# One core, attention, memory read and routed experts: row maxima written as the softmax shift, full-height bias products, expert numbers read a step earlier

## What is computed

```python
x = x + attn_a(layernorm(x))     # 16 query heads, 4 key groups, head size 16, causal softmax
x = x + ffn(layernorm(x))        # router, top 2 of 8 experts, 256 -> 176 -> 256
x = x + attn_b(layernorm(x))     # linear attention read from 4 memory banks
x = x + ffn(layernorm(x))        # the same experts again
```

```python
q = xh @ wq + bq ; k = xh @ wk + bk ; v = xh @ wv + bv     # biases are not zero
q, k = rmsnorm(q), rmsnorm(k)                              # then rotary embedding
logits = einsum(q, k) * head_scale ; causal mask
probs = softmax(logits) ; out = einsum(probs, v) @ wo + bo
```

## Time and profile before

| | us |
|---|---|
| median of 3 runs | 573.01 (572.78 to 574.89) |
| the profiled execution, its own time | 568.61 |
| its span, from first to last instruction | 566.8 |
| PE busy | 498.1 (88%) |
| DVE busy | 375.0 (66%) |
| ACT busy | 269.2 (47%) |
| POOL busy | 248.7 (44%) |

### The profile page before, as it was taken

The page is one execution under the profiler, slowest core; times in us unless marked ns, Lnnn a source line. Parts: engine busy times, 40 slices in busy tenths (PEclk is TensorE's granted clock), DMA queues, the critical chain, the costliest instruction groups (busy, mean ns, idle before and its releaser), DMA issues. The chain is left out here.

```text
span 566.8 us, 10974 instructions
## 1 busy us (share of the span) xinstructions
PE 498.1 (88%) x3374; PEld 336.2 (59%) x3374; DVE 375.0 (66%) x1098; ACT 269.2 (47%) x642; POOL 248.7 (44%) x308
## 2 busy tenths in 40 slices
PE   6899999889959969969999989999999787899970
PEld 2455666646736746746777656575667465677740
DVE  5989999779848936654443738766987373344473
ACT  4568998658846843423333333534134222233320
POOL 5329283466150052464243466237663453423440
PEclk9989999979988988989999988999999797999995
DMA  6480601110120231444323393212142244333496
GB/s 213 177 344 29 168 12 58 57 37 13 55 82 6 77 112 38 134 158 140 94 87 108 124 175 52 34 39 103 58 133 75 81 143 140 118 98 98 130 288 202
DMA packets 43736, 60.77 MB, mean 107 GB/s; under 512 B 5856, under 2 KB 38240, under 8 KB 43040
## 3 DMA queue, kind: packets, MB, share of 16 engines
q1 hardware_dynamic: 33152, 37.72, 21.9%
q0 software_dynamic: 9984, 21.83, 12.7%
q10 hardware_dynamic: 544, 0.52, 0.3%
HBM read 28.89 MB, written 25.00 MB: 95 GB/s over the span
## 5 line engine op out<-in xcount | busy, mean ns | idle before, releaser
L1917 POOL DMA_INDIRECT ys<-yo,xin x78 | 75.9, 973 | 126.3 <-DVE yo L1739 117.6
L1176 PE MATMUL PS<-wexp,xTt 128*128 x312 | 110.9, 483 | 8.5 <-ACT xTt L1382 6.8
L1518 DVE TENSOR_REDUCE smax<-PS 128x1 f32<-128x512 f32 (+3 forms) x176 | 103.2, 634 | 13.7 <-remote 7.9
L1344 ACT ACTIVATE prob<-PS 128x512 f16<-128x512 f32 (+1 forms) x176 | 92.1, 563 | 29.1 <-remote 13.3
L1902 POOL DMA_INDIRECT xs<-xn,pos x64 | 62.4, 976 | 59.0 <-DVE pos L1613 42.5
L1193 PE MATMUL PS<-wexp,hT 88*128 x312 | 83.6, 397 | 5.4 <-issue 3.0
L1726 DVE SCALAR_TENSOR_TENSOR sg<-th,PS 128x176 f32<-128x176 f32 x78 | 26.2, 336 | 80.6 <-ACT th L1388 65.3
L1176 PEld LDWEIGHTS PS<-wexp,xTt 128*128 128x128 f32 x312 | 56.9, 198 | 34.2 <-issue 13.7
L1388 ACT ACTIVATE th<-PS 128x176 f32<-128x176 f32 x78 | 24.7, 317 | 107.7 <-PE PS L1176 81.1
L1063 PE MATMUL PS<-qT,kbd 128*128 128x512 f16 (+3 forms) x256 | 63.7, 307 | 13.1 <-issue 7.6
L1193 PEld LDWEIGHTS PS<-wexp,hT 88*128 88x128 f32 x312 | 57.0, 197 | 18.0 <-issue 8.9
(11 more groups left out here) (210 smaller groups left out, 855.9 us busy)
## 6 DMA issues: line engine op xcount, KB each, us to landing
xin<-xs SPq DMA_DIRECT2D x78, 129.0 KB
wexp<-in_experts SPq DMA_DIRECT2D x4, 1216.0 KB, 9.1
kbd<-ys SPq DMA_DIRECT2D x18, 256.0 KB
xs<-zeros SPq DMA_DIRECT2D x32, 129.0 KB
xn<-xn SPq DMA_DIRECT2D x8, 512.0 KB, 3.4
xall<-ys POOLq DMA_DIRECT2D x6, 512.0 KB, 5.9
out<-xall SPq DMA_DIRECT2D x8, 256.0 KB
kbd<-kT SPq DMA_DIRECT2D x60, 32.0 KB, 1.9
```

What stands on the lines that cost most here:

```text
L1176: mm = pe.matmul(PS[:, bank, 0:2 * FI], xTt[:, j % NXT, kc * P:(kc + 1) * P], wexp[:, bass.ds(expert[f, j], 1), kc * 2 * FI:(kc + 1) * 2 * FI]
L1344: act.activation(prob[:, u % NPR, 0:nr * w], PS[:, bank, 0:nr * w], ACT.Exp, scale=ATT_SCALE)\
L1518: dve.tensor_reduce(smax[:, i, REP * g + r0:REP * g + r0 + nr], PS[:, bank, 0:nr * w].rearrange("p (r w) -> p r w", r=nr), AX.X, ALU.max). ...
L1917: pool.indirect_dma_start(ys[f], bass.IndirectOffsetOnAxis(xin[:, j % NXIN, D + 1:D + 2].bitcast(I32), axis=0), yo[:, j % NYO], None).then ...
```

## The change

1. The row maxima are written by the reduction itself, as float16, into column HD of `qa`. The step `shift`, its semaphore and `smax` are gone, and so is column HD + 1. So that the value fits, ScalarE scales the transposed queries by 1/16 in its copy to `qT1`, and the keys hold -16.0 in one column.
2. `shiftedT` waits for the 11 reductions of its group directly, by `out_of` for each unit.
3. The bias products take 128 rows: `top_h` (row 0 ones, the others zero) by a bias tile of 128 rows.
4. The registers with the expert numbers are loaded by `name_experts`: at the first tile of a stage ahead of `xT`, otherwise behind the `gate_up` before the fourth.
5. POOL's presets write `top_h` (two memsets instead of one), and one key column instead of two; `clear` clears one column.
6. The planner loses the `shift` steps; its costs of `qkv`, `project` and `gate_up` on PE are smaller; NUDGE has new values throughout, so that the orders of all engines are new.

```diff
-NUDGE = {("add", 0): 0.2, ("apply", 0): -0.8, ("apply", 1): 25.7, ...
+NUDGE = {("add", 0): 79.9, ("apply", 0): 24.9, ("apply", 1): -16.5, ...
...
-        w.add(PE, r(), 0.69, "qkv", b, i, ...
+        w.add(PE, r(), 0.5, "qkv", b, i, ...
...
-        w.add(DVE, t, 0.5, "shift", b, g, after=[(DVE, "first", b, g, n) for n in range(NU)],
-              behind=[(DVE, "shift", *divmod(NG * b + g - 1, NG))] * (b + g > 0))
         last = NG * b + g - 2
-        w.add(PE, t, 0.23, "shiftedT", b, g, after=[(DVE, "shift", b, g)]
+        w.add(PE, t, 0.23, "shiftedT", b, g, after=[(DVE, "first", b, g, n) for n in range(NU)]
...
-        w.add(PE, r(), 1.05, "project", b, n, ...
+        w.add(PE, r(), 0.66, "project", b, n, ...
...
-    w.add(PE, t(0), 1.19 + 0.3 * ((j - STAGES[n][1]) % 4 == 0), "gate_up", f, j, ...
+    w.add(PE, t(0), 1.19, "gate_up", f, j, ...
...
+                def name_experts(f, j):
+
+                    n = stage_of(j)
+                    i = j - STAGES[n][1]
+                    if i == 0:
+                        pe.wait_ge(plan_ready, (LAST + 1) * f + n + 1)
+                    for k, v in enumerate(nc.values_load_multi_w_load_instructions(
+                            plan[0:1, PLAN_E[n] + i:PLAN_E[n] + i + 4], ...
+                        expert[f, j + k] = v
...
-                        pe.matmul(PS[:, bank, 0:QKV], ones_h[0:1], bqkv_h[0:1], start=False, stop=True)\
+                        pe.matmul(PS[:, bank, 0:QKV], top_h[:], bqkv_h[:], start=False, stop=True)\
...
-                        pe.wait_ge(shift_ready, NG * b + g + 1)
+                        for n in range(NU):
+                            out_of(pe, "first", b, g, n)
                         bank = room(pe, kind, b, g)
...
-                            mm = pe.matmul(o, ones_h[0:1], bo_h[0:1], start=False, stop=True)
+                            mm = pe.matmul(o, top_h[:], bo_h[:], start=False, stop=True)
...
+                        if j == STAGES[stage_of(j)][1]:
+                            name_experts(f, j)
                         pe.wait_ge(xin_loaded[j % NXIN], 16 * loads_of(f, j))
...
                         mm.then_inc(filled[bank], 1)
+                        n = stage_of(j)
+                        if (j + 1 - STAGES[n][1]) % 4 == 0 and j + 1 < STAGES[n][2]:
+                            name_experts(f, j + 1)
...
-                                       bank16(bank)[:, 0:len(groups) * S], ACT.Copy).then_inc(taken[bank], 1)
+                                       bank16(bank)[:, 0:len(groups) * S], ACT.Copy, scale=1.0 / SHIFT)\
...
-                        dve.tensor_reduce(smax[:, i, REP * g + r0:REP * g + r0 + nr],
+                        dve.tensor_reduce(qa[:, b % 2, i, REP * g + r0:REP * g + r0 + nr, HD],
                                           PS[:, bank, 0:nr * w].rearrange("p (r w) -> p r w", r=nr),
                                           AX.X, ALU.max).then_inc(taken[bank], 1)
-                    elif kind == "shift":
-                        ...
-                        link(dve.tensor_scalar(qa[:, b % 2, :, hs, HD], smax[:, :, hs], -1.0 / SHIFT, None, ALU.mult))
-                        dve.scalar_tensor_tensor(qa[:, b % 2, :, hs, HD + 1], smax[:, :, hs], -1.0 / SHIFT,
-                                                 qa[:, b % 2, :, hs, HD], ALU.mult, ALU.subtract)\
-                           .then_inc(shift_ready, 1)
...
-                        pool.memset(ones_h[:], 1.0)
+                        pool.memset(top_h[:], 0.0)
...
-                        pool.memset(ka[:, :, :, HD:HD + 2], SHIFT)
+                        pool.memset(top_h[0:1], 1.0)
+                        pool.memset(ka[:, :, :, HD:HD + 1], -SHIFT)
...
-                        pool.tensor_copy(bqkv_h[:], first["bqkv"][0:1]).then_inc(bias_ready, 1)
+                        pool.tensor_copy(bqkv_h[:], first["bqkv"]).then_inc(bias_ready, 1)
```

More of the change, by code:

```diff
@@ L89 @@
 OUTPUT_BANKS = (5, 6)
[L94 to L129, removed]
-         ("values", 1): 268.5, ("values", 2): 1.7, ("values", 3): -8, ("weigh", 0): -29.6, ("weigh", 1): 21.5,
-         ("wgt", 0): 13.6, ("wgt", 3): 48.1, ("xT", 0): 304.5, ("xT", 1): 14.6}
@@ L280, in front @@
     for i in range(NT):
-        w.add(PE, r(), 0.69, "qkv", b, i, after=[(DVE if h else ACTE, "f_turn", b, h) for h in range(len(halves(b)))]
+        w.add(PE, r(), 0.5, "qkv", b, i, after=[(DVE if h else ACTE, "f_turn", b, h) for h in range(len(halves(b)))]
               + [(ACTE, "constants"), (POOL, "bias"), (POOL, "presets")]
@@ L372, in back @@
     for n in range(2):
-        w.add(PE, r(), 1.05, "project", b, n, after=[(ACTE, "outT", b), (ACTE, "out_weights")], behind=[(PE, "project", b, 0)] * n, banks=m,
+        w.add(PE, r(), 0.66, "project", b, n, after=[(ACTE, "outT", b), (ACTE, "out_weights")], behind=[(PE, "project", b, 0)] * n, banks=m,
               emptied=(DVE, "project", b, n))
@@ L965, in _ @@
                 expert = {}
+                def name_experts(f, j):
[4 more added lines that the diff above has]
+                    for k, v in enumerate(nc.values_load_multi_w_load_instructions(
+                            plan[0:1, PLAN_E[n] + i:PLAN_E[n] + i + 4], engines=[mybir.EngineType.PE], min_val=0, max_val=NE - 1,
+                            skip_runtime_bounds_check_because="the plan names one of the experts")[1]):
+                        expert[f, j + k] = v
                 for kind, *a in ORDER[PE]:
@@ L1161, in _ @@
                         f, j = a
-                        n = stage_of(j)
-                        i = j - STAGES[n][1]
-                        if i == 0:
-                            pe.wait_ge(plan_ready, (LAST + 1) * f + n + 1)
-                            if j == 0 and f == 0:
-                                pe.wait_ge(experts_loaded, 16 * NE // 2)
-                        if i % 4 == 0:
-                            for k, v in enumerate(nc.values_load_multi_w_load_instructions(
-                                    plan[0:1, PLAN_E[n] + i:PLAN_E[n] + i + 4], engines=[mybir.EngineType.PE], min_val=0, max_val=NE - 1,
-                                    skip_runtime_bounds_check_because="the plan names one of the experts")[1]):
-                                expert[f, j + k] = v
+                        if j == 0 and f == 0:
+                            pe.wait_ge(experts_loaded, 16 * NE // 2)
                         out_of(pe, "xT", f, j)
@@ L1331, in _ @@
                         act.activation(qT1[:, b % 2, groups[0]:groups[-1] + 1].rearrange("p g s -> p (g s)"),
-                                       bank16(bank)[:, 0:len(groups) * S], ACT.Copy).then_inc(taken[bank], 1)
+                                       bank16(bank)[:, 0:len(groups) * S], ACT.Copy, scale=1.0 / SHIFT)\
+                           .then_inc(taken[bank], 1)
                     elif kind == "shiftedT":
@@ L1881, in _ @@
                             pool.wait_ge(presets, 2)
[L1882 removed]
+                        pool.memset(qa[:, b % 2, :, :, HD:HD + 1], 0.0).then_inc(cleared, 1)
                     elif kind == "late":
```

56 lines of the change are left out of this document (43 added, 13 removed).

## The result

| | us |
|---|---|
| before, median (572.78 to 574.89) | 572.89 |
| after, median of 4 runs (556.12 to 597.45) | 560.26 |
| ratio, 95% interval | 0.9754 (0.9709 to 0.9798) |
| forecast, and its range | 567.0 (557 to 577) |
| profiled execution after, its own time and span | 559.93, 558.1 |

The run of 597.45 was a disturbed one and is not in the ratio. The gain is 12.6 us by these medians and 14.1 by the ratio, where 6.0 were forecast: the direction and the range hold, but the forecast size is less than half of what came. The two traces are 8.7 us apart, since the traced execution of before was 4.4 us under its median. What follows compares times by ratios to the kernel before on the same chip, because chips differ (the median of before was 566.05 on one and 572.63 on another).

The account below looks back on a forecast made before the run. VectorE was taken to bound the scores, TensorE the expert rounds' gate/up products. 4.1 + 1.8 + 0.6 (shift) + 1.1 (bias) - 1.6 (waits) = 6.0 us, so the median 573.0 becomes 567.0, range 557 to 577.

Parts of the forecast that it names:

- The bound: Scores from 35 to 105 us: VectorE sets the pace at 96% busy, ScalarE next; TensorE's 67.81 us flatters it.
- Rival A: From 35 to 158 us TensorE or ScalarE already paces, absorbing freed time: gain 1, 572 us; chance 0.22 together with D.
- The shift step: VectorE's queue gets back 9.9 us; on the path 4.1 (35 to 105 us), 1.8 (120 to 158), 0.6 elsewhere.
- The reduction into float16: VectorE's row-maximum reductions writing float16: taken as 0, bounds 0 and 7.0 us more on VectorE.
- rival D: Each reduction into float16 costs 40 ns, returning 7.0 of 9.9 us: gain 1, 572 us; chance 0.22 together with A.
- The bias products: 128-row bias products in the `qkv` and output projections: 0.2 us each, 6.5 us of TensorE, 1.1 on the path.
- The waits: TensorE's waits for 11 units ahead of each `shiftedT`: a cost of 0.1 us each, 1.6 us, ends 0 and 9.6.
- Rival B: Sequencer has no lead at `shiftedT`, so waits hold TensorE 0.6 us per group, +9.6: slower, 577.6 us; chance 0.15.
- The register loads: Expert-number loads ahead of gate/up products: already hidden, taken as 0; what can be won is 0 to 1.6 us.
- The new order: New queue orders of all engines: taken as 0 because the steps are the same, with plus and minus 4 us.
- rival C: The new order is much better, two holds near the scatters don't occur: gain 14, 559 us; chance 0.15.
- The test that was to reveal the order: If a stage without edited steps (memory read, last round) changes by more than 3 us, the order did it.

Follow-up runs that it names:

- x3: The kernel before, in its old order, with only the shift step taken out (reduction writes float16, `shiftedT` waits for 11 units): ratio 1.0022 to the kernel before.
- x1: The kernel before, in its old order, with only the bias products made 128 rows high: ratio 0.9974 to the kernel before.
- x0: The changed kernel measured again, unaltered, on a second chip: ratio 0.9739 to the kernel before.
- z2: The changed kernel with batch 0's scatters spread and batch 1's eight spaced, with six small memsets between scatters: ratio 0.9531 to the kernel before.
- y1: The changed kernel with batch 0's eight scatters put back in a row on POOL: ratio 0.9847 to the kernel before.
- w1: The kernel before, old order and none of the edits, with batch 0's and 1's scatters spaced by memsets and a few moved: ratio 0.9753 to the kernel before.

## Why the prediction was half right

**The bound.** From 35 to 105 us VectorE was called the fullest engine and TensorE's 67.81 a flattering figure. x3 shows that it wasn't flattering enough to be set aside: with VectorE at 64.80 nothing was won. Rival A (the freed time is absorbed) was right for this edit alone.

**The shift step**: forecast 6.5 us on the path, less 1.6 for the waits, so 4.9; alone (x3) the kernel came out 1.3 us slower, within 0.5% of none. The 4.1 us for the stretch from 35 to 105 us rested on VectorE setting its pace alone, and that failed. VectorE's own saving was mis-sized too: its busy time fell by 7.5 us, not 9.9 to 11. The reductions didn't take over the dear waits, as the Trainium skill has it (SBUF — State Buffer, "Who interferes with whom"), and this case agrees: 634 ns before, 639 in x3, 637 in the changed kernel. A small `tensor_scalar` step took longer instead: the one that makes `n_veps` took 4.8 us in all before, 5.6 in x3 and 6.3 in the changed kernel. That is 1.5 of the 3.9 us by which the saving in the changed kernel fell short of the 11.4 removed.

**The reduction into float16**: 0, right; the bound of 7.0 and rival D fall, as 637 ns stand against 634.

**The bias products**: 0.2 us each, 6.5 us of TensorE, of which 1.1 on the path. The pauses are as forecast, and x1 alone gives 1.5. The rule that a product of 32 rows takes the time of one of 128 (the Trainium skill, TensorE: Matmul & The Clock Gate, "Why this matters for your kernels") doesn't carry over to these one-row products, the only low ones here: 0.27 against 0.16 us to the next start. But together with the shift they are worth 3.3 us where the two alone add up to 0.2, which a share on the path for each edit couldn't say.

**The waits**: 1.6 us forecast, 2.6 of TensorE measured, eleven waits against three. Against the single wait of before it can't be read off, since there TensorE also waited for the shift itself. Rival B (9.6) falls: the visible part is 0.16 a group.

**The register loads**: 0 forecast, some 2 to 4 likely, open.

**The three edits together**: 6.0 us forecast, 5.7 and 7.1 measured. That the sum came out was luck: the term for the shift was too large, those for the bias and perhaps the loads too small, and the gain came from the edits acting together, which no term held.

**The new order** is the step that failed: "I take 0: the steps are the same". It measured 8.2 us alone, and by the ratios 1.2 to 1.6%, some 7 to 9 us, on top of the edits. The plus and minus 4 was too narrow as well. That alone makes the forecast gain less than half of the measured one. The prediction had the row before its eyes: 3.92 us of VectorE idle with no releaser, within a run of eight scatters; rival C named two such holds, 559 us, and gave them 0.15. What was missing was to ask which bit of the order lengthens or shortens such a run, and to look for it in POOL's list of both kernels: six, one and one instead of eight. The test that was to reveal the order (a stage without edited steps changing by over 3 us) could not see it, since the rows of batches 0 and 1 lie among the scores, where the edits are. The last round, from its first `xT` to its last `down`, did change by 3.8 us (123.0 to 126.8), but it takes 126.5 in x1 too, where the order is the old one.

**Left open.** What in a run of indirect DMAs slows the other engines (1.43 us from start to start where POOL issues every 1.27) isn't shown; that it goes when 0.9 to 1.5 us of other work stand between them is. POOL's issuing by itself is not the whole of it, as the pauses last some 1.5 us beyond the end of its last scatter. The transfers are a rival that no run parts from it: from 145 to 155 us the DMA engines are busy 26% in x0 and 21% in z2, and TensorE does 58 products there and 120. Which part of its price is the pause and which the lower clock behind it wasn't separated. How much of the order's 8.2 us lies outside batch 0's row wasn't tried beyond y1, whose 6 us have an interval of some 4.

## What to carry to other kernels

Look in the trace for stretches where all engines idle with no releaser, and at what the one busy engine repeats there: here eight back-to-back scatters instead of six, one and one cost some 6 us, more than any single edit brought, and small fillers or other work between them gave 14 us to the untouched kernel. When two engines are both near full, price edits on both together: each alone measured from a loss of 1.3 to a gain of 1.5 us, all together 6 to 7. An order planned anew is an edit of its own: compare the lists of every engine, the idle ones' too, around each run of repeated DMAs.

## What the runs showed of the hardware

A run of scatters (0.96 us each, one per 1.27) on POOL slows the other engines to a step every 1.4 us (seen in y1), from some 4 us behind its start to some 1.5 us behind its end, and TensorE's granted clock was 0.77 from 105 to 120 us; with 1.5 us of memsets between them (0.9 in w1), neither is seen. A sequencer's wait takes 51 ns and the next stands 0.11 us on; three ahead of a product are hidden (77.3 us of the kernel before), and eleven semaphores waited for instead of three show 0.16 us on average. A product with a one-row operand delays its successor by 0.1 us against one of 128 rows (0.27 and 0.21 against 0.16 and 0.11 us). A reduction from PSUM takes as long with a float16 result as with a float32 one (637 and 634 ns).
